# A Macaron layer with two mixture-of-experts halves: the copies that go to the experts are listed ahead of all pieces of the first expert's weight split

## The reference, cut to what matters

```python
def _L0_ffn_ref(x, gate_w, sw1, sw2, sw3, rw1, rw2, rw3):
    y = _swiglu(xf, sw1, sw2, sw3)                      # shared expert, 704 wide
    scores = jax.nn.softmax(xf @ gate_w, axis=-1)
    weights, indices = jax.lax.top_k(scores, TOPK)      # 2 of 8 experts for each token
    cw = jnp.zeros((N, E)).at[jnp.arange(N)[:, None], indices].add(weights)
    for e in range(E):
        h = _swiglu(xf, rw1[e], rw2[e], rw3[e])         # 352 wide
        y = y + cw[:, e:e + 1] * h
    return y.reshape(B, T, D)
x = x + 0.5 * _L0_ffn_ref(_layernorm(x), ...)
x = x + _L0_attn_ref(_layernorm(x), Wq, Wk, Wv, Wo)
x = x + 0.5 * _L0_ffn_ref(_layernorm(x), ...)
```

## Time and profile before

| | us |
|---|---|
| median of 3 runs | 1592.67 |
| lowest and highest | 1591.82, 1602.43 |
| the profiled execution | 1591.82 |
| its span (first to last instruction) | 1590.0 |
| mean granted clock of TensorE in it | 0.988 |

### The profile page before, as it was taken

How to read it: one execution, slowest core, us unless ns; L and a number is a source line. 1 busy time by engine, 2 the same in 40 slices (tenths; PEclk the granted TensorE clock), 3 DMA queues, 4 the chain that set the end, 5 groups by cost and what they waited for, 6 DMA issues and landing times.

```text
span 1590.0 us, 23990 instructions
## 1 busy us (share of the span) xinstructions
PE 1537.4 (97%) x8100; PEld 1113.6 (70%) x8100; DVE 915.3 (58%) x1558; ACT 647.4 (41%) x968; POOL 910.9 (57%) x753
## 2 busy tenths in 40 slices
PE   8999999999997899999999999999999999999997
PEld 7777799999876774444444444327778889999985
DVE  5554433333378686777777777786555443333336
ACT  4422232332332315666666666672541223323321
POOL 4106396506667857788878888840313558633754
PEclk9999999999998998999999999999999999999999
DMA  9306555425272331212111111114102555544446
GB/s 349 139 1 229 196 195 191 150 82 193 99 219 73 91 73 43 34 29 44 38 30 40 41 31 30 19 32 167 60 1 89 186 192 208 171 138 139 146 130 214
DMA packets 123041, 180.15 MB, mean 113 GB/s; under 512 B 33968, under 2 KB 74800, under 8 KB 120624
## 3 DMA queue, kind: packets, MB, share of 16 engines
q1 hardware_dynamic: 109664, 104.43, 22.3%
q0 software_dynamic: 12832, 73.67, 13.3%
q10 hardware_dynamic: 432, 0.54, 0.1%
HBM read 106.48 MB, written 55.97 MB: 102 GB/s over the span
## 4 chain that ended last, share of the span: by engine, by line
PE 79%; DVE 6%; issue 3%; ACT 3%; POOL 3%; DMA 2%; SPq 2%; another core or an unknown queue 1%; DVEq 0%; POOLq 0%; ACTq 0%
PE PS L1243 10%; PE PS L1245 10%; PE PS L1244 10%; PE PS L1466 7%; PE PS L1480 7%; PE PS L1447 6%; PE PS L1372 3%; PE PS L1375 3%; PE PS L1374 3%; PE PS L1377 3%; PE PS L1373 3%; PE PS L1376 3%; PE PS L1496 3%; PE PS L1387 2%; SPq L1179 1%
## 5 line engine op out<-in xcount | busy, mean ns | idle before, releaser
L1734 ACT ACTIVATE PT<-PS 128x1024 f32<-128x1024 f32 x256 | 258.0, 1024 | 125.9 <-PE PS L1466 122.4
L2047 DVE TENSOR_REDUCE nmf_later<-PS 128x1 f32<-128x1024 f32 x160 | 194.1, 1219 | 59.0 <-PE PS L1447 58.7
L1480 PE MATMUL PS<-PT,V 128*32 128x512 f32 x1024 | 202.9, 605 | 0.0
L2124 POOL TENSOR_TENSOR W<-raw,W 128x544 fp32r<-128x544 f32 x144 | 190.7, 1359 | 1.5
L1466 PE MATMUL PS<-QS,KS 98*128 98x512 f32 x512 | 178.5, 432 | 4.6 <-DVE nmf_later L2047 3.7
L1029 POOL TENSOR_TENSOR added<-PT 128x1024 f32<-128x1024 f32 x56 | 136.4, 2436 | 76.5 <-ACT PT L1734 76.5
L1466 PEld LDWEIGHTS PS<-QS,KS 98*128 98x128 f32 x512 | 85.5, 191 | 129.1 <-issue 49.1
L1447 PE MATMUL PS<-KS,QS 96*128 96x512 f32 x512 | 169.1, 412 | 3.5 <-DVE nmf_first L2047 1.6
L2012 DVE TENSOR_TENSOR thid<-thid,PS 128x352 f32<-128x352 f32 x78 | 40.7, 521 | 197.5 <-ACT thid L1665 197.5
L2155 POOL DMA_INDIRECT x_routed<-xq,pos x64 | 67.9, 1061 | 137.9 <-issue 115.0
L1243 PE MATMUL PS<-xh,W 128*128 128x512 f32 x352 | 140.7, 400 | 5.4 <-DVE xl L1761 2.1
(11 more groups left out here) (207 smaller groups left out, 3815.3 us busy)
## 6 DMA issues: line engine op xcount, KB each, us to landing
raw<-ffn_w POOLq DMA_DIRECT2D x18, 2176.0 KB, 10.2
y_routed<-ytile SPq DMA_DIRECT2D x78, 256.0 KB
xn<-x_routed SPq DMA_DIRECT2D x160, 64.0 KB, 2.1
x_routed<-xq SPq DMA_DIRECT2D x1, 9984.0 KB, 29.5
xs<-x_routed SPq DMA_DIRECT2D x152, 64.0 KB, 2.2
QS<-later_hi SPq DMA_DIRECT2D x112, 64.0 KB, 2.0
raw<-ffn_w SPq DMA_DIRECT2D x6, 768.0 KB, 6.2
raw<-ffn_w SPq DMA_DIRECT2D x16, 272.0 KB
```

Of the source, the lines that this page charges most:

```text
L1480: e.matmul(PS[i * QUARTER:(i + 1) * QUARTER, ob, :], V[:, b * QT + kt, g, :], PT[:, part_of_unit(u), kt % 2 * GRP:(kt % 2 + 1) * GRP], sta ...
L1734: e.activation(PT[:, part_of_unit(u), :], PS[:, i:i + 2, :].rearrange("p b n -> p (b n)"), ACT.Exp, scale=SCALE).then_inc(p_ready.sem, 1)
L2047: e.tensor_reduce(row_maxima(n)[:, h, t:t + 1], PS[:, i:i + 2, :].rearrange("p b n -> p (b n)"), AX.X, ALU.max, negate=True).then_inc(max_ ...
L2124: low = e.tensor_tensor(W[:, slot, 1, cs], raw[slot][:, cs], W[:, slot, 0, cs], ALU.subtract)
```

## The change

The slots of `beside` are listed in another order. All eight tiles 0 to 7 come one slot after the other, without the slots of `first_split` between them; `first_load` hangs on the last of them (tile 7); and the four slots of `first_split` follow. Number and kinds of slots are the same, and so is the loop that takes them.

```diff
-        sent = [[("rows", s, t), ("scatter", s, t)] for g in ORDER[1:] for t in group_tiles(g)]
-        sent[TPG - 1].append(("first_load", s))
-        beside.extend(sent[:TPG])
-        for i in range(0, SPLITS, 2):
-            beside.extend(sent[TPG + i:TPG + i + 2] + [[("first_split", s, i), ("first_split", s, i + 1)]])
+        beside.extend([("rows", s, t), ("scatter", s, t)] for g in ORDER[1:] for t in group_tiles(g))
+        beside[-1].append(("first_load", s))
+        beside.extend([("first_split", s, i), ("first_split", s, i + 1)] for i in range(0, SPLITS, 2))
```

## The result

The changed kernel took 1606.78 us (median of 14 runs, 1599.52 to 1610.01), the kernel before 1597.12 us (14 runs, 1589.45 to 1602.5) beside it: ratio 1.0056, 95% interval 1.004 to 1.0073. Of the 14.3 us between 1592.5 and 1606.78, 4.6 are the median of before, 1597.12 here and 1592.67 over its first three runs; 9.7 are the change. The profiled execution took 1601.98 us, span 1600.1, 10.1 us more than before's span.

The account below looks back on a forecast made before the run. TensorE, busy 97% of the span, was taken as the bound. All terms were 0 against 1591.82 us, giving 1591.8, stated as 1592.5 because the runs' median is 0.85 us higher; range from 1589 less 1 us to 1600.

Parts of the forecast that it names:

- The copies, waits and gates on DVE: First FFN, steps 13 to 16: copies wait for scatters, but gates still come before TensorE asks for them; cost 0.
- The load of expert 0: On SP, the load still begins at about 124 us despite its later slot; worth 0.
- The end of the dispatch: First FFN: POOL's last scatter is over near 165.2 us and landed at 167 instead of 172.6; worth 0.
- Pieces, second FFN, first tile's place: Late pieces and the second FFN cost 0; the first transposition in the first FFN stays near 177.6 us.
- POOL's pace: Moving pieces from beside POOL's DMAs leaves its pace by the page, or saves 0.33 us a meeting by the row.
- The sum is 0 by both: Verdict on POOL's pace: whether page or row holds, moving the pieces changes the total time by 0.
- A stall comes: Rival: mirror stall of TensorE, as the second FFN's scatters run closer together; same price slower, 1595.5; chance 0.10.
- Gates held up by the sending: Rival: late-landing scatters make copy 7 block step 15's gate; some 5 us in each FFN, 1602; chance 0.06.
- The stall goes: Rival: the new order removes TensorE's stall before 161.66 in the first FFN; 3.2 us faster, 1589; chance 0.10.
- The upper end, 1600: Top of the range: mirror stall and first held-up gates give 1597, plus a few us for the median's spread.

Follow-up runs that it names:

- g4: Changed kernel's order of copies, but one piece of expert 0 beside each copy of tiles 0 to 7; ratio to before 1.0002.
- g2: The changed kernel itself, run again beside the kernel before; ratio 1.0052.
- i1: Changed kernel, scatters of the first FFN sending only the first half of each row; ratio to before 1.0063.
- g1: The kernel before, unchanged, run again for its trace; ratio 0.9985.
- g3: Changed kernel with POOL waiting ahead of tiles 4, 8 and 12 in each FFN until the tile before has landed; ratio to before 0.9997.
- f4: Changed kernel with a small memset by POOL ahead of each scatter's DMA; ratio to before 1.0132.
- e4: Kernel before, with POOL waiting ahead of tiles 4, 8 and 12 until the tile before has landed; ratio to before 1.0001.
- e3: Changed kernel with POOL waiting ahead of tiles 4, 8 and 12 until the tile before has landed; ratio to before 1.0001.
- f2: Changed kernel with one pause of POOL, ahead of tile 4 in the first FFN until the tile before has landed; ratio to before 1.0002.
- groups 1, 3 and 5: Follow-up runs, each group on one chip beside the kernel before, which took 1588.68, 1596.29 and 1596.04 us.
- i2: Changed kernel with 500 already met waits on SP, behind the load of expert 0 in the first FFN; ratio to before 1.0058.
- groups 2 and 4: Follow-up runs, each group on one chip beside the kernel before, which took 1579.64 and 1579.88 us.
- e1: Changed kernel's order of copies, but one piece of expert 0 beside each copy of tiles 0 to 7; ratio to before 1.0007.
- f1: The changed kernel itself, run again beside the kernel before; 1580.21 us, ratio 1.000.

## Why the prediction was wrong, step by step

- **The copies, waits and gates on DVE:** right. Copies 2, 4 and 5 were to wait 1.1, 2 and 2 us and waited 1.02, 1.91 and 2.02; the gate of step 13 was to start at 143.2 and started at 142.85. The gate of step 14 was to start at 151.3 and started at 152.80, because of TensorE's signal (recorded at 152.71) and not of copy 5, over at 150.71. Copy 7's wait of 2.5 to 3 us didn't come, since that late gate stood ahead of it.
- **The load of expert 0:** right, 123.78. **The end of the dispatch:** right, POOL's last DMA was over at 164.30 for 165.2 worked out, and SP loaded 1.83 us behind it, for the 1.8 us taken.
- **Pieces, second FFN, first tile's place:** the second FFN was right, 70.97 and 70.98 us (one copy waited 1.60 us there, for "next to none"). The first transposition, "still near 177.6", came at 185.20, by the stall.
- **POOL's pace:** the row was right against the inference beside it, and its worth was misjudged. Away from the pieces the DMA at 142.19 takes 0.97 us, and 1.42 at 156.49 beside them. "The sum is 0 by both" looked only at the waits of the copies: g4 and g2 are 1.41 and 1.29 us for a DMA and 0.5% of the time apart. Whether the pace makes that difference isn't shown, as pace alone wasn't varied.
- **The step that failed** is the rival "A stall comes", put at 0.10 and +3.2 us, and what was held against it: "TensorE's own work is the same, and POOL sends scatters 14 to 5 ... at the same times as before". The mechanism is this one, a stall with nothing shown. It was mis-sized, since it was priced as a copy of the one in the earlier trace rows (1.44 + 1.7 is 3.1 and not 3.2): it came to some 8 us in the first FFN (7.6 to 7.9 us of idle time in g2 and i1, 6.96 in the profiled execution, in place of 1.44). And it was mis-weighed, since POOL's stream was read only for when it ends. From 138 us on before sent sixteen DMAs in a row, starts 1.36 us apart, as three of them took 1.30 to 1.44 us beside pieces or the gate's low part, and then paused for copy 6; the changed kernel sends twenty, 1.31 us apart on average. That is what the change did to POOL's stream, and TensorE's work it left alone. But the four more DMAs are not the whole cause. The lateness had grown before they came: the signal of step 14's second half was 0.96 us late in before (end at 149.24; 0.98 in g1) and 3.79 us here (148.92). By then both streams had started nine DMAs, 1.32 and 1.29 us apart. So what in the new order makes the signals later, at nearly the same stream, stays open; that the stream is needed for it is shown by g3.
- **Gates held up by the sending** (0.06) did not happen by the mechanism named, late landings: in the profiled execution TensorE has no wait for a gate before the stall. In g2 it waits 0.66 us for DVE's product at 156.94, but DVE had waited for TensorE's late signal. f4 shows the form of a gate that is late by the copies.
- **The stall goes** (0.10): not by this change, but by pauses, with a stretch of 57.41 us in e4 and 56.87 in g3, where g1 has 59.48, without a gain in the time that can be measured.
- **The upper end, 1600:** even with before's first median the ratio gives 1592.67 x 1.0056 = 1601.6.

The trace of before held the hint in two rows that I read for the idle time and not for its releaser: DVE's 7.12 us at 161.85 by "remote" beside TensorE's 0.81 us at 161.66 by "issue". POOL had sent without a pause for 21 us just ahead of both.

## What to carry to other kernels

A wait put down to "remote" for a signal of the core's own engine is a symptom: look when the sender was done, and what else was being sent. Closing up a stream of indirect DMAs can cost more than it gives, even where every wait is hidden; short pauses in it cost nothing that could be measured in five runs of three kernels (e3, e4, f2 and two repeats), and three pauses in each FFN took back 0.5% where the changed kernel lost it. And when a change is worth less than a per cent, measure it in more than one group: here it was 1.0056, 1.0052, 1.000 and 0.9995.

## What the runs showed of the hardware

- **Late signals.** In the first measurement and in groups 1, 3 and 5 TensorE's semaphore updates came up to 15 us after the matmul, and TensorE then stopped issuing, during streams of indirect DMAs 1.28 to 1.41 us apart. ACT's and DVE's gate signals were in time, and SP's already met waits came 0.5 us apart for 0.06 (i2). In groups 2 and 4 the same stream delayed none by over 0.02 us, which also says that the modelled ends of matmuls are good enough for this comparison.
- **A state of the surroundings, not of the program.** Before took 1596 to 1597 us where g2 or its like stalled, 1580 us where not, and 1588.68 in group 1, where signals are up to some 8 us late (e1) and the changed kernel didn't run. Of these 16 us the first dispatch explains some 3.6, if before takes the 55.8 us of the changed kernel there (its own stretch is known only where signals are late, 59.45 and 59.48). Groups 2 and 3 carry the same chip number and are of different kinds. What differs isn't known.
- **Missing records.** Where signals came late, the profile lacks semaphore records: 20,237 to 20,630 of them in the 12 traces of such groups, 21,955 to 22,024 in the 8 of groups 2 and 4. Of the 1652 that the changed kernel's profile lacks against f1's, 1561 are of landed DMAs; instructions are lacking in neither (23,990 each). The Trainium skill, "NOTIFIC — the notification-queue block", in "Overflow: three behaviours, one of which stalls the engine", has it that the inner pipeline of the block that writes such records pushes back when it fills, rather than lose one, and that a full ring in memory may, by its setting, drop new records. Late signals, stopped issue and SP's slow waits would fit the first, missing records the second; no run tells whether either happened. If it is so, part of the loss belongs to the recording; every run here has its granted clock on record, and none tells what the kernel does without recording. Open too is which count matters, descriptors or packets, as half rows left the rows and DMAs as they were, while their packets in the 20 us fell from 1133 to 768.
- **Pieces and POOL.** The Trainium skill, "SBUF — State Buffer", in "Who interferes with whom", infers that such a tensor_tensor doesn't hold up descriptor generation. The rows say otherwise: in the changed kernel the DMA from 156.49 on, with nothing but pieces on DVE beside its start, took POOL 1.42 us for 0.97, while those beside copies alone (140.91, 142.19) took 0.97; in g4 the excess is up to 0.90 us. The measurement decides.
